# One pool of seven PSUM banks, the next batch's queries made beside attention, and its first sixteen row maxima spread over both feed-forward stretches

## The chip, the cores and the metric

The kernel runs on one core of a Trainium2 chip. The core has five engines with instruction streams of their own: TensorE (PE in the profile; its weight loads are shown as PEld), VectorE (DVE), ScalarE (ACT), GpSimd (POOL) and SyncE (SP), which here only starts DMAs. Each engine takes its instructions strictly in the order in which they were written; engines meet only through semaphores. PSUM is the memory that TensorE writes into; it has eight banks of 128 partitions x 512 float32. The metric is device time in microseconds (us) for one launch, lower is better.

## The reference, cut to what matters

Two transformer layers over 8 batches of 256 rows x 128 features. Everything is float32.

```python
# per batch b: x [256,128], ctx [1601,128], idx [256,64] in 0..255
x = x + xattn0(layernorm(x), ctx)       # 16 heads of width 8, softmax over 1601 keys
x = x + ffn0(layernorm(x))              # 9 experts of 352 hidden, sigmoid gate, top 2
x = x + xattn1(layernorm(x), ctx, idx)  # q rows attend to 64 of the first 256 latent keys each
x = x + ffn1(layernorm(x))              # 8 experts of 176 hidden, softmax gate, top 2, one shared expert
# expert: silu(x @ w1.T) * (x @ w3.T) @ w2.T, weighted per row; all experts are computed for all rows
# attn:   softmax((q * 8**-0.5) @ k.T) @ v, then an output projection
```

## The kernel before, in words

**Layer 0 attention.** Keys and queries are split into bfloat16 parts and stacked on 48 (+3) rows, so that one bfloat16 matmul gives a float32-like score. Heads are taken in pairs (p = 0 to 7), one on partitions 0 to 63 and one on 64 to 127. First the row maximum of the scores is needed. For each pair the 256 queries x 1601 keys are cut into 8 pieces, `max_part` makes the scores of a piece for both heads in two neighbouring banks (event `part`, 64 per batch, L566), and VectorE reduces both banks in one instruction (L1031). After the eighth piece of a pair VectorE takes the minimum (negated maxima), GpSimd splits it into three bfloat16 parts and writes them into the query stack `qst` (L1156 to L1159), TensorE transposes the pair's queries again (event `q0`, L535), and only then are the real scores made, keys on partitions: event `s0` (`scores`, L581, two banks, 56 per batch), exp on ScalarE (L838), weighted sum of the values in bank `ob` (event `w0`, L595), then `ev0` and `c0`.

**Layer 1 attention** does the same with 256 keys and a count mask: `pair1`, `q1`, `s1`, `mu`, `w1`, `c1` for each head pair. The counts come from `df` (GpSimd, L1197), `eq` (VectorE, L1057) and `cnt` (TensorE, L740).

**Feed-forward.** 27 chunks (layer 0) and 14 chunks (layer 1) of up to 128 hidden rows. `gu` puts the gate and up products of a chunk into the two halves of one bank (L652, L653); ScalarE makes tanh and a copy (L844, L814); VectorE makes (tanh+1)*gate and frees the bank (event `hd`, L1043); GpSimd multiplies by the up half into `hid` (L1191). `dn` (L663) multiplies an expert's hidden rows by its down weights, and VectorE adds the weighted result to x (L1049).

**What is prepared for the next batch.** `ctx`, `key`, `val`, `lat`: transposed context, keys, values. Key parts are written to DRAM and read back into the stack `kst`, two head pairs at a time (event `rel` on SyncE, L485, semaphore `kst_in0` to `kst_in3`). `n4`, `n4a`, `xT4`, `pq0`: the first layernorm, transpose and projection of the queries; VectorE makes their high parts, GpSimd the low parts (L1147 to L1150). `idx`: GpSimd turns the row indices into the form that `df` needs (L1134 to L1141). `all0` (L529): all queries transposed into `qa`, the operand of the maxima.

**What sets the order.** `order()` gives every event a time on an abstract axis and sorts; all engines walk the one sorted list and issue their share of each event. A batch takes R = 87.35 units: attention of batch b from 0 to 56 together with layer 1 attention of batch b-1; layer 1 feed-forward of b-1 from Y1 = 55; layer 0 feed-forward of b from Y0 = 65.5 to about 86. The times only set an order; they are not waits.

**Banks.** Events that ScalarE reads (`F_NEED`: `s0`, `s1`, `q0`, `q1`, `c0`, `cnt`, `ctx`, `key`, `val`, `all0`, ...) take the three banks `b0` to `b2` in strict rotation; `free_fill(e)` waits until the user three places earlier has been read. Events that VectorE reads (`M_NEED`: `part`, `pair1`, `dn`, norm transposes, ...) and `gu` take the four quarters of `um`, placed by a small planner, and `free_slot` waits for the last user. `f_read` counts ScalarE's reads, `u_read` VectorE's. In the program before, a chunk `gu` of batches 2 to 6 takes its bank a median of 2 places after the event that frees it, and a least of 1; `s0` a median of 5 and a least of 1; `part` a median of 7 and a least of 2 (places in the sorted list, all events counted).

## Time and profile before

| | us |
|---|---|
| median of 3 runs | 2027.4 (2025.6 to 2028.34) |
| profiled execution, whole | 2015.62 |
| its span | 2013.8 |
| TensorE busy | 1657.3 (82%) |
| VectorE, ScalarE, GpSimd busy | 1027.6, 985.7, 960.3 |
| mean granted TensorE clock | 0.89 of full speed |

The profile names a line of the kernel, the engine, the operation and output<-inputs with buffer numbers left out (`b` for b0 to b2; `big` is one tile that holds many small ones). "Idle before" is the time that the engine sat idle just before the instruction, and what ended it. Times inside one batch are read from the period that begins at 1126 us: layer 1 feed-forward until 1157, layer 0 feed-forward until 1218, attention until 1359; the next period begins there.

### The profile page before, as it was taken

The page shows a single profiled execution, that of the slowest core. Times are in us where ns is not written, and L with a number is a line of the kernel's source. Part 1 is how long each engine was busy: PE and PEld are TensorE (multiplying, and loading weights), DVE is VectorE, ACT ScalarE, POOL GpSimd, SP SyncE. Part 2 cuts the span into 40 slices and gives each one's busy share as a digit, 9 for nine tenths or more (in the row PEclk, how much of TensorE's full clock was granted, in tenths as well). Part 3 has the DMA queues.
Part 4 walks back from the last instruction along what each step waited for, and adds up shares of the span by engine and source line. Part 5 has one row for each costly group of instructions (what it writes and reads, how often), then busy time and mean ns, then how long its engine had stood idle before and what let it go on. Part 6 is the DMA issues. An engine that isn't in the chain of part 4 may idle for free.

```text
span 2013.8 us, 35829 instructions
## 1 busy us (share of the span) xinstructions
PE 1657.3 (82%) x13006; PEld 889.9 (44%) x13006; DVE 1027.6 (51%) x2124; ACT 985.7 (49%) x2543; POOL 960.3 (48%) x1529
## 2 busy tenths in 40 slices
PE   3488778898788988889888987889788997889667
PEld 3233543356333753347433563337533474336425
DVE  3355365545654556535665456545565446645313
ACT  2256436653467435663366445564366533663222
POOL 0345335644366345645357354654457453653342
PEclk8589888899799998889889997889988998999857
DMA  6300400021000200011000200002000200000000
GB/s 180 94 9 18 81 1 9 18 58 27 1 17 19 76 1 1 25 40 47 1 9 18 62 24 1 17 20 74 1 2 25 49 18 1 1 11 6 1 1 3
DMA packets 64863, 53.74 MB, mean 27 GB/s; under 512 B 14762, under 2 KB 57140, under 8 KB 64692
## 3 DMA queue, kind: packets, MB, share of 16 engines
q1 hardware_dynamic: 64692, 51.47, 10.2%
q8 instruction: 107, 1.75, 0.4%
q14 instruction: 64, 0.52, 0.1%
HBM read 38.98 MB, written 12.46 MB: 26 GB/s over the span
## 4 chain that ended last, share of the span: by engine, by line
PE 66%; ACT 10%; DVE 9%; POOL 8%; issue 5%; SPq 1%; DMA 1%; ACTq 0%; POOLq 0%; DVEq 0%
PE um L663 10%; PE ob L595 10%; PE um L652 7%; PE b L581 7%; PE um L566 6%; PE um L653 5%; ACT probs L838 4%; DVE mx L1031 3%; PE b L541 3%; PE b L621 2%; ACT big L814 2%; ACT big L889 2%; POOL hid L1191 2%; PE um L608 2%; PE b L637 2%
## 5 line engine op out<-in xcount | busy, mean ns | idle before, releaser
L1031 DVE TENSOR_REDUCE mx<-um 128x2 f32<-128x802 f32 (+1 forms) x512 | 502.3, 991 | 351.6 <-PE um L566 346.5
L838 ACT ACTIVATE probs<-b 128x512 f32<-128x512 f32 (+1 forms) x896 | 458.6, 564 | 185.4 <-PE b L581 176.1
L1191 POOL TENSOR_TENSOR hid<-hid,th 128x256 f32<-128x256 f32 (+3 forms) x328 | 237.5, 728 | 408.1 <-DVE th L1043 406.4
L844 ACT ACTIVATE th<-um 128x256 f32<-128x256 f32 (+3 forms) x328 | 125.6, 383 | 404.3 <-PE um L653 386.7
L595 PE MATMUL ob<-probs,vaug 128*9 128x256 f32 (+1 forms) x3328 | 305.6, 420 | 0.0
L1197 POOL TENSOR_TENSOR big<-iotab,idx_lo 128x512 bf16<-128x512 bf16 x256 | 267.6, 1058 | 23.0 <-PE b L740 16.6
L581 PE MATMUL b<-big,kst 64*128 64x256 bf16 (+1 forms) x1664 | 188.0, 299 | 83.5 <-ACT big L889 36.2
L566 PE MATMUL um<-kst,qa 64*128 64x401 bf16 (+1 forms) x1024 | 193.1, 375 | 14.6 <-DVE mx L1031 12.1
L814 ACT ACTIVATE big<-b 128x256 bf16<-128x256 bf16 (+3 forms) x280 | 104.5, 380 | 189.8 <-PE b L535 110.1
L1043 DVE SCALAR_TENSOR_TENSOR th<-th,um 128x256 f32<-128x256 f32 (+3 forms) x328 | 135.2, 414 | 102.6 <-ACT hid L814 100.4
L652 PE MATMUL um<-xnT,w1T 128*128 128x256 f32 (+1 forms) x432 | 143.1, 414 | 34.8 <-DVE th L1043 20.0
L1049 DVE SCALAR_TENSOR_TENSOR x<-um,cw,x 128x128 f32<-128x128 f32 x288 | 87.7, 346 | 164.5 <-PE um L663 164.5
L581 PEld LDWEIGHTS b<-big,kst 64*128 64x128 bf16 (+1 forms) x1664 | 64.8, 98 | 184.5 <-ACT probs L838 62.2
L663 PE MATMUL um<-w2T,hid 128*128 128x128 f32 (+1 forms) x864 | 118.2, 289 | 27.8 <-POOL hid L1191 27.8
L653 PE MATMUL um<-xnT,w3T 128*128 128x256 f32 (+1 forms) x432 | 130.5, 384 | 0.0
L663 PEld LDWEIGHTS um<-w2T,hid 128*128 128x128 f32 (+1 forms) x864 | 109.8, 201 | 39.0 <-DVE th L1043 31.5
L814 ACT ACTIVATE hid<-um 128x256 f32<-128x256 f32 (+3 forms) x328 | 123.8, 377 | 0.0
L663 PE MATMUL um<-wd_sb,hid 128*128 128x128 f32 (+1 forms) x576 | 121.3, 318 | 1.9 <-POOL hid L1191 1.9
L566 PEld LDWEIGHTS um<-kst,qa 64*128 64x128 bf16 x1024 | 52.1, 98 | 154.6 <-issue 73.0
L1221 POOL TENSOR_TENSOR big<-big 128x512 f32<-128x512 f32 (+2 forms) x40 | 35.6, 889 | 165.5 <-ACT big L814 165.5
L1119 DVE TENSOR_REDUCE mx<-um 128x4 f32<-128x1024 f32 x64 | 78.3, 1223 | 66.4 <-PE um L612 65.6
L1233 POOL TENSOR_TENSOR big<-big,sq_nat 128x512 f32<-128x512 f32 x64 | 80.2, 1274 | 57.3 <-ACT big L889 57.3
(203 smaller groups left out, 2293.1 us busy)
## 6 DMA issues: line engine op xcount, KB each, us to landing
kst<-k_parts SPq DMA_DIRECT2D x384, 50.0 KB
k_parts<-big SPq DMA_DIRECT2D x72, 128.0 KB, 1.9
ctx_sb<-in_ctx SPq DMA_DIRECT2D x8, 768.0 KB
k1st<-k_parts SPq DMA_DIRECT2D x96, 32.0 KB
k_parts<-big SPq DMA_DIRECT2D x24, 64.0 KB, 1.6
kst<-in_L_ffn_w SPq DMA_DIRECT2D x1, 1408.0 KB
x<-in_x SPq DMA_DIRECT2D x8, 128.0 KB, 2.3
out<-x SPq DMA_DIRECT2D x8, 128.0 KB, 1.8
```

Of the source, the lines that this page charges most:

```text
L566: m = pe.matmul(own[hh][:, 0:n], qa[o:o + SLOT, p, s, :], kst[o:o + SLOT, p, j * KM:j * KM + n], start=True, stop=True)
L581: m = pe.matmul(own[hh][0:kn, (c % 2) * NQ:(c % 2 + 1) * NQ], kst[o:o + SLOT, p, c * P:c * P + kn], qp[o:o + SLOT, p % 2, :], start=True, ...
L595: m = pe.matmul(ob[q:q + V1, 0:NQ], vaug[b % 2][0:kn, c, 2 * p + hh, :], probs[0:kn, (2 * (NGB * b + g) + hh) % NPS, (c % 2) * NQ:(c % 2 + ...
L652: pe.matmul(g[0:n, 0:NQ], wa, xnT[l][:, :], start=True, stop=True)
L653: pe.matmul(g[0:n, NQ:2 * NQ], wb, xnT[l][:, :], start=True, stop=True).then_inc(gu_ready, 1)
L663: m = pe.matmul(bank[:, s * P:(s + 1) * P], hid[r0:r1, (NCH * b + u) % NHID, s * P:(s + 1) * P], w[r0:r1, at, :], start=(k == 0), stop=(k ...
L814: return act.activation(o, i, ACT.Copy)
L838: act.activation(probs[0:kn, (2 * own + hh) % NPS, 0:w], bs[(e + hh) % 3][0:kn, 0:w], ACT.Exp).then_inc(f_read, 1)
L1031: dve.tensor_reduce(mx[:, p % 2, s, :, j], pair[:, :, 0:w], AX, ALU.max, negate=True).then_inc(u_read, 1)
L1043: dve.scalar_tensor_tensor(out=t, in0=t, scalar=1.0, in1=g[0:nr, 0:NQ], op0=ALU.add, op1=ALU.mult).then_inc(u_read, 1)
L1191: pool.tensor_tensor(hid[0:nr, own % NHID, :], hid[0:nr, own % NHID, :], th[0:nr, own % NTH, :], ALU.mult).then_inc(hid_ready, 1)
L1197: m = pool.tensor_tensor(onehot[:, own % 2, q:q + QG, :], iotab[:, :].unsqueeze(1).to_broadcast([P, QG, P]), idx_lo[:, QG * n:QG * (n + 1) ...
```

## The change

Four edits go together.

1. `um` has 3584 columns, seven banks, and `b0` to `b2` are gone. One planner walks the sorted list and gives every event the bank or banks whose last user was released longest ago; an event that needs two banks for one VectorE instruction (`part`, `pair1`) must get neighbours. A bank counts as ready when its last user's event (for `gu`: its `hd`) lies earlier in the list. `free_bank` then waits on `f_read`, on `u_read`, or on both, for the last users of just these banks.
2. `n4`, `n4a`, `xT4`, `pq0`, `all0` and `idx` of the next batch move from the layer 0 feed-forward (Y0+1.0 to Y0+9.7) into attention (36.2 to 51.5).
3. The first 16 maxima of the next batch (12 before) are spread evenly from Y1+1.4 = 56.4 to 84.9, one per 1.90 units; before, the 12 came one per 0.82 units from 77.4 on. The other 48 come one per 0.896 units from 0.1 on (52, one per 0.82, before).
4. ScalarE's reads take the bank from the plan.

By the new plan `gu` takes its bank a median of 7 places after the event that frees it (least 6), `s0` 6 (least 4), `part` 6 (least 3), `s1` 6 (least 5; before 3, least 2). Of the 56 `s0` of batch 4, 26 now wait for a VectorE read too, and of all events that waited only for ScalarE's reads 51 do; of its 64 `part` 29 now wait for a ScalarE read.

```diff
-        um = psum("um", 2048)
-        bs = [psum(f"b{k}", 512) for k in range(3)]
+        um = psum("um", 512 * NBANK)
...
+        EARLY = 16
+        EARLY_STEP = (R - 2.4 - Y1 - 1.4) / (EARLY - 1)
...
-                for d, kind in ((1.0, "n4"), (2.5, "n4a"), (3.3, "xT4"), (4.6, "idx"), (4.8, "pq0"), (12.1, "lat")):
-                    put(prep + Y0 + d, kind, b)
+                for d, kind in ((36.2, "n4"), (37.8, "n4a"), (38.6, "xT4"), (45.6, "pq0"), (51.5, "idx"), (Y0 + 12.1, "lat")):
+                    put(prep + d, kind, b)
-                    put(prep + Y0 + 9.1 + 0.6 * n, "all0", b, n)
+                    put(prep + 50.2 + 0.7 * n, "all0", b, n)
-                    put(own - 9.9 + 0.82 * k if k < 12 else own + 0.82 * (k - 12) + 0.1, "part", b, k)
+                    put(prep + Y1 + 1.4 + EARLY_STEP * k if k < EARLY else own + (43.0 / (NH0 - EARLY)) * (k - EARLY) + 0.1, "part", b, k)
...
+            need = F_NEED.get(kind, 0) or M_NEED.get(kind, 0) or int(kind == "gu")
...
+            ready = [k for k in range(NBANK) if since(k) < at[ev]]
+            if kind in M_NEED and need == 2:
+                own = min(([k, k + 1] for k in ready if k + 1 in ready), key=lambda r: max(since(k) for k in r))
+            else:
+                own = sorted(ready, key=since)[:need]
+            place[ev] = own
+            before = [last[k] for k in own if last[k] is not None]
+            f_free[ev] = max([fill[v] + F_NEED[v[0]] for v in before if v in fill], default=0)
+            u_free[ev] = max([rel[v] + 1 for v in before if v not in fill], default=0)
...
-            def free_fill(e):
-                if e >= 3:
-                    pe.wait_ge(f_read, e - 2)
-                return bs[e % 3][:, :]
-
-            def free_slot(ev):
+            def free_bank(ev):
+                if f_free[ev] > 0:
+                    pe.wait_ge(f_read, f_free[ev])
                 if u_free[ev] > 0:
                     pe.wait_ge(u_read, u_free[ev])
                 return quarter[place[ev][0]]
```

Three places of the order. TensorE, in the second half of the layer 0 feed-forward of batch 4, before; one expert is three chunks `gu` (w1T, w3T) and one `dn` (w2T), and `um<-kst,qa` is a maximum of the next batch:

```order
1933 L652 MATMUL um<-xnT,w1T 96x256
1934 L653 MATMUL um<-xnT,w3T 96x256
1935 L566 MATMUL um<-kst,qa 128x401 x2
1936 L652 MATMUL um<-xnT,w1T 128x256
1937 L653 MATMUL um<-xnT,w3T 128x256
1938 L566 MATMUL um<-kst,qa 128x401 x2
1939 L652 MATMUL um<-xnT,w1T 128x256
1940 L653 MATMUL um<-xnT,w3T 128x256
1941 L566 MATMUL um<-kst,qa 128x401 x2
1942 L663 MATMUL um<-w2T,hid 128x128 x6
```

The same engine and stretch now:

```order
1948 L662 MATMUL um<-xnT,w1T 96x256
1949 L663 MATMUL um<-xnT,w3T 96x256
1950 L576 MATMUL um<-kst,qa 128x401 x2
1951 L662 MATMUL um<-xnT,w1T 128x256
1952 L663 MATMUL um<-xnT,w3T 128x256
1953 L662 MATMUL um<-xnT,w1T 128x256
1954 L663 MATMUL um<-xnT,w3T 128x256
1955 L673 MATMUL um<-w2T,hid 128x128 x6
```

One maximum stands in each expert instead of three in the last four experts. GpSimd in the layer 0 feed-forward of batch 4, before, with `idx` and the low parts of the next queries between two chunks' products:

```order
748 L1191 TENSOR_TENSOR hid<-hid,th 96x256
749 L1134 TENSOR_SCALAR idx_f<-idx_t 128x128
750 L1137 CAST idx_c<-idx_f 64x128
751 L1138 TENSOR_SCALAR idx_c<-idx_t 64x128
752 L1137 CAST idx_c<-idx_f 64x128
753 L1138 TENSOR_SCALAR idx_c<-idx_t 64x128
754 L1140 TENSOR_SCALAR idx_f<-idx_f 128x128
755 L1141 TENSOR_TENSOR idx_lo<-idx_t,idx_f 128x128
756 L1147 CAST qst<-qres 128x32x8
757 L1148 TENSOR_TENSOR qst<-qres,qst 128x32x8
758 L1149 COPY qst<-qst 128x32x16
759 L1150 COPY qst<-qst 128x32x8
```

GpSimd now, at the end of attention of batch 4; the last rows of `key` (L1231 to L1235) and `df` (L1207) stand between them:

```order
726 L1207 TENSOR_TENSOR big<-iotab,idx_lo 128x512 x2
727 L1157 CAST qst<-qres 128x32x8
728 L1158 TENSOR_TENSOR qst<-qres,qst 128x32x8
729 L1159 COPY qst<-qst 128x32x16
730 L1160 COPY qst<-qst 128x32x8
731 L1231 TENSOR_TENSOR big<-big 128x256
732 L1233 CAST big<-big 128x256
733 L1235 TENSOR_TENSOR big<-big 128x256
734 L1207 TENSOR_TENSOR big<-iotab,idx_lo 128x512
```

The low parts now stand ahead of the last key of the batch, whose parts go to DRAM. TensorE at the start of the layer 1 feed-forward (wg_sb, wu_sb), beside the last sums of attention, before:

```order
3881 L652 MATMUL um<-xnT,wg_sb 128x256 [waits u_read]
3882 L653 MATMUL um<-xnT,wu_sb 128x256
3883 L595 MATMUL ob<-probs,vaug 9x256 [waits f_read]
3884 L595 MATMUL ob<-probs,vaug 9x256 x3
3885 L652 MATMUL um<-xnT,wg_sb 128x256 [waits u_read]
3886 L653 MATMUL um<-xnT,wu_sb 128x256
```

And now:

```order
3203 L662 MATMUL um<-xnT,wg_sb 128x256 [waits f_read]
3204 L663 MATMUL um<-xnT,wu_sb 128x256
3205 L605 MATMUL ob<-probs,vaug 9x256 [waits f_read]
3206 L605 MATMUL ob<-probs,vaug 9x256 x3
3207 L576 MATMUL um<-kst,qa 128x401 [waits f_read,kst_in0]
3208 L576 MATMUL um<-kst,qa 128x401
3209 L662 MATMUL um<-xnT,wg_sb 128x256 [waits f_read]
```

The first maximum of the next batch, with its wait for the first key stack, stands here now; before it stood about 21 units later. (The two excerpts are of different batches; the pattern is the same in each.)

## Rows read from the trace of the kernel before

**Rows 1.** The page, parts 1 and 4: busy time, and the last chain by engine.
```profile
PE 1657.3 (82%) x13006; PEld 889.9 (44%) x13006; DVE 1027.6 (51%) x2124; ACT 985.7 (49%) x2543; POOL 960.3 (48%) x1529
...
PE 66%; ACT 10%; DVE 9%; POOL 8%; issue 5%; SPq 1%; DMA 1%; ACTq 0%; POOLq 0%; DVEq 0%
```
**Rows 2.** Windows: length, busy of PE, PEld, DVE, ACT, POOL, clock, DMA share, GB/s.
```profile
1126.00:1157.00 31.00, 30.64 (x166) 21.16 (x158) 16.81 (x74) 11.15 (x35) 9.39 (x13) 1.00 0.35 75
1157.00:1218.00 61.00, 51.90 (x305) 39.55 (x306) 32.73 (x77) 22.16 (x62) 30.28 (x48) 0.97 0.07 20
1218.00:1359.00 141.00, 118.38 (x1108) 46.31 (x1109) 76.06 (x108) 86.07 (x214) 80.18 (x128) 0.83 0.04 13
```
**Rows 3.** Waits of PE, whole run: waiting <- releaser: us, times, longest.
```profile
PE b L535 <- POOL qst L1159: 43.4, 24, 2.5
PE b L581 <- ACT big L889: 36.2, 43, 1.0
...
PE um L663 <- POOL hid L1191: 29.8, 23, 2.8
...
PE um L652 <- DVE th L1043: 20.4, 37, 1.4
...
PE b L581 <- ACT probs L838: 16.9, 46, 0.5
PE b L581 <- ACTq L866: 15.4, 19, 1.4
PE b L621 <- ACT probs L838: 15.0, 26, 0.8
PE um L652 <- DVE x L1049: 14.8, 21, 0.7
PE um L566 <- DVE mx L1031: 12.1, 18, 1.1
```
**Rows 4.** Waits of PE's weight loads, whole run.
```profile
PEld b L581 <- ACT probs L838: 62.2, 119, 0.9
...
PEld b L581 <- ACT big L889: 46.3, 43, 1.3
```
**Rows 5.** Timeline, layer 0 feed-forward: start, us, engine, line, operation.
```profile
1169.35 0.54 POOL L1134 TENSOR_SCALAR idx_f<-idx_t 128x128 f32<-128x128 f32 x1
...
1175.91 2.77 POOL L1191 TENSOR_TENSOR hid<-hid,th 128x256 f32<-128x256 f32 x4
...
1178.14 1.58 PE L663 MATMUL um<-w2T,hid 128*128 128x128 f32 x12 [2.81 <-POOL hid L1191]
```
**Rows 6.** Timeline, attention: a pair's maximum ready, its transpose.
```profile
1053.68 0.22 POOL L1159 TENSOR_TENSOR qst<-nmr,qst 128x4 bf16<-128x4 f32 x1
...
1054.04 0.27 PE L535 MATMUL b<-identb,qst 128*128 128x128 bf16 x2 [0.91 <-POOL qst L1159]
```
**Rows 7.** The page, part 5: a maximum on VectorE.
```profile
L1031 DVE TENSOR_REDUCE mx<-um 128x2 f32<-128x802 f32 (+1 forms) x512 | 502.3, 991 | 351.6 <-PE um L566 346.5
```
**Rows 8.** Tile kst from 1110 to 1200 us: issues, ns min/median/max, first and last start.
```profile
L485 SPq DMA_DIRECT2D kst<-k_parts x48: 265/298/593, 1123.8 to 1140.1; - x48
```
**Rows 9.** The page, part 6: DMA issues and KB each.
```profile
kst<-k_parts SPq DMA_DIRECT2D x384, 50.0 KB
...
k1st<-k_parts SPq DMA_DIRECT2D x96, 32.0 KB
```
**Rows 10.** Windows of that stretch, columns as in Rows 2.
```profile
1119.00:1124.00 5.00, 4.19 (x50) 2.11 (x46) 2.06 (x10) 3.79 (x10) 0.70 (x1) 1.00 0.25 71
1124.00:1130.00 6.00, 5.69 (x56) 2.45 (x53) 2.91 (x22) 4.12 (x11) 0.73 (x1) 1.00 0.51 104
```
**Rows 11.** Timeline of PE and PEld in the layer 1 feed-forward.
```profile
1129.12 0.62 PE L595 MATMUL ob<-probs,vaug 128*9 128x256 f32 x8
...
1154.36 0.41 PEld L653 LDWEIGHTS um<-xnT,wu_sb 128*128 128x128 f32 x2
...
1154.79 1.65 PEld L663 LDWEIGHTS um<-wd_sb,hid 128*128 128x128 f32 x8
```

More of the change, by code:

```diff
@@ L156, in build @@
         cw = [sb("cw0", [P, NS, NE]), sb("cw1", [P, NS, NE])]
-        um = psum("um", 2048)
-        bs = [psum(f"b{k}", 512) for k in range(3)]
+        um = psum("um", 512 * NBANK)
         ob = psum("ob", 512)
-        quarter = [um[:, 512 * k:512 * (k + 1)] for k in range(4)]
+        quarter = [um[:, 512 * k:512 * (k + 1)] for k in range(NBANK)]
         def sem(name):
@@ L367, in build, with since @@
                 serial[ev] = (group, 1 + sum(1 for g in serial.values() if g[0] == group))
-        seen, last = 0, [-1] * 4
+        at = {ev: k for k, ev in enumerate(EV)}
+        given = {ev: at["hd", ev[1], ev[2]] if ev[0] == "gu" else at[ev] for ev in EV}
+        last = [None] * NBANK
+        f_free, u_free = {}, {}
         for ev in EV:
             kind = ev[0]
-            if kind in M_NEED or kind == "gu":
-                need = M_NEED.get(kind, 1)
-                at = [range(k, k + need) for k in range(5 - need) if max(last[k:k + need]) < seen]
-                own = min(at, key=lambda r: (kind == "gu" and last[r[0] ^ 1] < seen, max(last[k] for k in r)))
-                u_free[ev] = max(last[k] for k in own) + 1
-                place[ev] = list(own)
-                for k in own:
-                    last[k] = rel[ev]
-            if kind in M_NEED or kind == "hd":
-                seen += 1
+            need = F_NEED.get(kind, 0) or M_NEED.get(kind, 0) or int(kind == "gu")
+            if not need:
+                continue
+            def since(k):
+                return -1 if last[k] is None else given[last[k]]
+            ready = [k for k in range(NBANK) if since(k) < at[ev]]
[3 more added lines that the diff above has]
+                own = sorted(ready, key=since)[:need]
+            assert len(own) == need, ev
+            place[ev] = own
+            before = [last[k] for k in own if last[k] is not None]
+            f_free[ev] = max([fill[v] + F_NEED[v[0]] for v in before if v in fill], default=0)
+            u_free[ev] = max([rel[v] + 1 for v in before if v not in fill], default=0)
+            for k in own:
+                last[k] = ev
         count = {ev: n for ev, (group, n) in serial.items()}
@@ L570, in scores @@
                 p, j = divmod(g, NG)
-                e = fill["s0", b, g]
                 if j == 0:
                     pe.wait_ge(f_read, fill["q0", b, p] + 1)
-                own = [free_fill(e), free_fill(e + 1)]
+                free_bank(("s0", b, g))
+                own = [quarter[k] for k in place["s0", b, g]]
                 if b == 0:
@@ L616, in scores1 @@
             def scores1(b, p):
-                e = fill["s1", b, p]
                 pe.wait_ge(f_read, fill["q1", b, p] + 1)
-                own = [free_fill(e), free_fill(e + 1)]
+                free_bank(("s1", b, p))
+                own = [quarter[k] for k in place["s1", b, p]]
                 for hh in range(2):
@@ L724, in _ @@
                 elif kind == "all0":
-                    bank = free_fill(fill[ev])
+                    bank = free_bank(ev)
                     pe.wait_ge(qst_ready, b + 1)
@@ L728, in _ @@
                 elif kind == "q0":
-                    bank = free_fill(fill[ev])
+                    bank = free_bank(ev)
                     pe.wait_ge(m_ready, NP * b + n + 1)
@@ L742, in _ @@
                 elif kind == "xT4":
-                    bank = free_slot(ev)
+                    bank = free_bank(ev)
                     pe.wait_ge(ln_ready, norm_no("n4", b))
@@ L759, in _ @@
                 elif kind == "aT0":
-                    bank = free_slot(ev)
+                    bank = free_bank(ev)
                     pe.wait_ge(at_ready, b + 1)
@@ L763, in _ @@
                 elif kind == "o0":
-                    bank = free_slot(ev)
+                    bank = free_bank(ev)
                     pe.wait_ge(u_read, rel["aT0", b, 0] + 1)
@@ L779, in _ @@
                 elif kind == "all1":
-                    bank = free_fill(fill[ev])
+                    bank = free_bank(ev)
                     pe.wait_ge(qst1_ready, b + 1)
@@ L797, in _ @@
                 elif kind == "aT1":
-                    bank = free_slot(ev)
+                    bank = free_bank(ev)
                     pe.wait_ge(at1_ready, b + 1)
@@ L801, in _ @@
                 elif kind == "o1":
-                    bank = free_slot(ev)
+                    bank = free_bank(ev)
                     pe.wait_ge(u_read, rel["aT1", b, 0] + 1)
@@ L827, in _ @@
                     e = fill[ev]
-                    bank = bs[e % 3][:, :]
+                    bank = quarter[place[ev][0]]
                     act.wait_ge(f_psum, e + 1)
@@ L837, in _ @@
                         act.wait_ge(f_psum, e + hh + 1)
-                        act.activation(probs[0:kn, (2 * own + hh) % NPS, 0:w], bs[(e + hh) % 3][0:kn, 0:w], ACT.Exp).then_inc(f_read, 1)
+                        act.activation(probs[0:kn, (2 * own + hh) % NPS, 0:w], quarter[place[ev][hh]][0:kn, 0:w], ACT.Exp).then_inc(f_read, 1)
                 elif kind == "gu":
```

45 lines of the change are left out of this document (23 added, 22 removed).

## The prediction

> **What bounds the kernel now.** I read the page first, then the windows of one batch, then who waited for whom on TensorE.
>
> The page shows no engine near its limit but TensorE: busy 82% of the span, the other three 48 to 51%, and the chain that ended last runs through TensorE for 66% of the span [rows 1]. So the question is what makes TensorE stand idle. The three windows of one batch (233 us) answer where: layer 1 feed-forward is dense (30.6 of 31 us busy), layer 0 feed-forward is idle for 61 - 51.9 = 9.1 us, attention for 141 - 118.4 = 22.6 us [rows 2]. The batch has 200.9 us of busy TensorE and 32.1 us of idle. The granted clock is 1.00 and 0.97 in the feed-forward windows and 0.83 in attention.
>
> The waits say why. Seven rows are waits for a bank: scores for ScalarE's exp and copies (36.2, 16.9, 15.4 us), layer 1 scores (15.0), feed-forward chunks for VectorE (20.4, 14.8), maxima for VectorE (12.1); together 130.8 us [rows 3]. They go with places in the order: a chunk's bank is freed one or two events before it is taken, a score's sometimes one. Two rows are waits for data: a pair's queries for GpSimd's maximum parts (43.4) and the down product for GpSimd's hidden rows (29.8) [rows 3].
>
> **The change part by part.** The sum is over the whole run and against the profiled execution's own 2015.6 us; the median of the runs is 2027.4, 11.8 higher, and I carry the difference over to it.
>
> *Seven banks in one pool.* At most the 130.8 us of idle go, if nothing else is late. The weight loads show that each such wait also lays bare the tail of the matmul before it: for the scores they waited 62.2 + 46.3 = 108.5 us where the matmuls' rows of the same two releasers show 16.9 + 36.2 = 53.1 [rows 3, 4]. With the whole of the scores' three wait rows (68.5) set against 108.5, the factor is 1.58, and the upper end is 130.8 x 1.58 = 207 us. The lower end is below nothing, since scores now also wait for VectorE (the rival below). After the change every kind has 6 to 7 events between free and take, at 2.5 us per score group in attention (141 us for 56) the six events are more than one group, about 3 us, against 1 us for a maximum on VectorE [rows 7] and twice 0.6 for the exps. That holds most of the time, not always, because ScalarE and VectorE also run in order and some waits will come back as waits for data a little later. I take 0.7 of the idle: -92 us.
>
> *Maxima spread.* Before, the last maximum of pair 1 (k = 15) stood at 0.82 x 3 + 0.1 = 2.6 units and the pair's queries at 2.8; pair 2's at 9.1 against 9.8. VectorE, four GpSimd steps and a semaphore had to fit between them, and TensorE waited: in the row at 1054 us it starts 0.14 us after GpSimd's last step ended [rows 6]. Now pair 1 is done before attention starts, pair 2 at 6.4 against 9.8, pair 7 at 42.2 against 44.8: always 2.6 units or more, 6 us. The 43.4 us [rows 3] go except for a rest; I take -40 (ends -20 and -43). The four maxima that leave attention are the same work elsewhere: no change in the sum of TensorE.
>
> *Next queries beside attention.* In the feed-forward GpSimd spends 1169.35 to 1175.91, 6.6 us, on `idx` and the low parts while four chunk products pile up behind it; the down product waits 2.81 us for them [rows 5]. Eight times 2.8 is 22 us of the 29.8; I take -20 (ends 0 and -22). In attention the same 6.6 us lie beside other work: GpSimd is busy 80 of 141 us there [rows 2], and all queries are needed 4.6 units after the projection. TensorE's transposes and projection only change place. If that cover were gone, the next `all0` would wait, at most 6.6 us a batch.
>
> *The first maximum waits for the stack.* `kst` of the first two pairs is read back by 12 DMAs that start at 1123.8, behind 12 of `k1st` [rows 8]. Together these are 12 x 32 + 12 x 50 = 984 KB [rows 9]; the traffic from 1119 to 1130 is 71 x 5 + 104 x 6 = 979 KB [rows 10]. So the stack is there at about 1130.0 or a little later. The new first maximum stands behind the sum at 1129.12 [rows 11], so about 1129.7: 0.3 us early. Moreover the low parts now stand ahead of the last key on GpSimd, and the reload hangs on that key. If none of it shifts, the wait is 0.3; if the whole 6.6 us block came before the key it would be 6.9. Both engines meet work there that partly overlaps, so I take 1.5 us a batch, +12 us (ends 0 and +55). Behind the waiting matmul stand all chunks of the dense layer 1 feed-forward, and VectorE's `hd` behind the missing maximum.
>
> *Five maxima inside the layer 1 feed-forward.* TensorE has no idle there [rows 2]; VectorE has 14 us. A 0.99 us maximum [rows 7] that stands in front of an `hd` can make a down product late. One of five does, I assume: 1.0 x 8 = +8 us (ends 0 and 5 x 0.99 x 8 = +40).
>
> *A second semaphore.* Some 50 scores and other fills a batch now wait for two. A down product has always waited for two: at 1154.79 its weights load 0.02 us after the load before it ended (1154.36 + 0.41) [rows 11]. I take 0; a tenth of a us each would be +40.
>
> Sum: -92 - 40 - 20 + 12 + 8 = -132 us: 1883.6 for the profiled execution, 1895 for the median. Per batch it is 16.5 us of the 32.1 idle. The layer 0 feed-forward window should go from 61 to about 52 us: up to 9.1 of idle there, less what returns, and the queries' projection and transposes moved out.
>
> **The rivals.**
>
> *The waits only change their names.* Every score still needs its exp before the sum, and ScalarE, VectorE and GpSimd take 86, 76 and 80 of attention's 141 us in order [rows 2]. If that chain sets the pace, a score that starts earlier only waits in front of the sum. Then only the feed-forward's bank waits go (20.4 + 14.8 = 35), half of the 43.4 and the 20, against +20: -57, 1970. For it: layer 1's chain of eight steps per pair is fixed latency. Against it: no engine there is over 61% busy, and the scores' waits name the bank's reader, not the data.
>
> *The clock comes back.* Attention has 0.83, so about 34% of its time at 1.2 GHz and the rest at 2.4 (0.66 + 0.34/2), and the feed-forward windows, where TensorE hardly pauses, have 0.97 to 1.00 [rows 2]. The clock fell where pauses are many. If the pool closes most of them, up to 48 us a batch run at full clock; with TensorE busy for 84% of it, half of 40 us is saved at most, and other engines take half of that again: 10 us a batch, -80 on top, 1815. Against it: sums that are short for the array remain, so pauses remain. The Trainium skill, "TensorE: Matmul & The Clock Gate", section on psum-queue depth-cycling, tells of a kernel that cycles through PSUM banks with small idles between matmul groups, whose clock swings between the two levels and whose throughput falls; by it fewer waits for banks would give this result. The trace agrees in that clock and idle go together by window.
>
> *Slower: scores held by maxima.* One pool ties ScalarE's banks to VectorE's. In a batch 51 events that waited for ScalarE alone now wait for a VectorE read as well. If VectorE lags more than a score group behind (a norm, a routing block, `eq` in a row), each holds TensorE for up to one maximum, 0.99 us [rows 7]: 50 us a batch at most. Set against it, what the change takes away is (130.8 + 43.4 + 22) / 8 = 24.5 us a batch, so it decides from 25 of the 51 on. At 31 it costs 6 us a batch more than is gained: 2075. Against it: VectorE is busy for 54% of attention and waited 346.5 us for maxima itself [rows 2, 7], so it is usually ahead.
>
> **How the numbers follow.** My forecast has 0.62, from its terms between 1840 and 1950. The renamed waits have 0.17 (1970, 1950 to 2015), the returning clock 0.10 (1815), the slower case 0.11 (2075). The range 1825 to 1990 leaves out the slower case, a piece of the renamed waits and a piece of the clock's, together 2 in 10. A difference under 0.2% (4 us) is about what a measurement of this kernel can't tell from none. Faster by more: 0.62 + 0.10 + 0.14 of the 0.17 = 0.86; within: 0.03; slower: 0.11.
>
> **What would show it.** In the profile after: the waits of scores (now L591) for ScalarE and VectorE together under 40 us, of pair queries (L548) for GpSimd under 5, of chunks (L662) for VectorE under 10; the layer 0 feed-forward window at 50 to 54 us; the first maximum waiting for a DMA of `kst` for 0 to 3 us in each batch; TensorE's busy sum per batch near 200 us, unless the clock changes. The prediction is wrong if waits of the sums (L605) for exps grow by as much as the scores' fall, if scores wait for `mx` for tens of us, or if attention stays at 140 us.

## The result, and the profile after

The changed kernel takes 1903.66 us (median of 3 runs, 1889.44 to 1908.15) against 2027.4: a ratio of 0.9375, 95% interval 0.9297 to 0.9453. The forecast was 1895. Times further down are medians that leave out an execution over 1.5% above the fastest of its kernel. The profiled execution spans 1901.8 us. The page after, answering to [rows 1]:

```profile
PE 1616.2 (85%) x13006; PEld 884.1 (46%) x13006; DVE 1023.9 (54%) x2124; ACT 971.0 (51%) x2543; POOL 957.6 (50%) x1529
...
PE 60%; POOL 10%; DVE 9%; ACT 8%; issue 5%; SPq 4%; DMA 3%; POOLq 0%; ACTq 0%; DVEq 0%
```

The span fell by 112 us, in two parts: TensorE's idle from 2013.8 - 1657.3 = 356.5 to 1901.8 - 1616.2 = 285.6 (-71), and its busy time by 41, though it does the same 13006 matmuls. A DMA has come onto the chain (3%, with SyncE's queue 4%). The windows of one batch, answering to [rows 2]; lengths differ since the stages were cut at their first chunks:

```profile
1061.00:1100.00 39.00, 34.22 (x176) 22.84 (x169) 21.11 (x77) 11.40 (x37) 9.46 (x13) 0.91 0.24 66
1100.00:1148.00 48.00, 45.68 (x268) 35.16 (x268) 27.41 (x63) 19.40 (x57) 20.34 (x31) 1.00 0.09 25
1148.00:1285.00 137.00, 120.03 (x1175) 49.60 (x1173) 76.87 (x124) 89.39 (x224) 89.64 (x145) 0.86 0.05 15
```

One batch is a sample; for comparisons I cut every profile at the first and last layer 0 chunk and the first layer 1 chunk and took the mean over six batches. "Slow" is the time at 1.2 GHz that the mean granted clock c stands for, length x 2(1 - c); c is read to two digits, so it is good to about half a us.

| kernel | layer 1 feed-forward | layer 0 feed-forward | attention | of it idle | of it slow | batch |
|---|---|---|---|---|---|---|
| before | 31.3 | 55.4 | 144.4 | 24.8 | 36.4 | 231.1 |
| after | 39.2 | 47.6 | 130.8 | 16.8 | 23.5 | 217.6 |

So the two feed-forward stages nearly cancel (+7.9 and -7.8), and what is left is attention (-13.6), of whose gain 8.0 us are idle and up to half of 12.9 the clock. TensorE's waits after, answering to [rows 3]:

```profile
PE um L576 <- DMA kst<-k_parts: 38.2, 8, 6.9
PE um L673 <- POOL hid L1201: 32.7, 18, 3.1
...
PE um L647 <- POOL big L1243: 23.8, 18, 3.5
...
PE um L554 <- ACT oT L824: 20.9, 27, 1.5
PE um L548 <- POOL big L1169: 16.0, 16, 2.5
PE um L591 <- DVE mx L1041: 15.2, 18, 1.2
PE um L618 <- ACT probs L848: 9.9, 18, 0.8
...
PE um L591 <- ACT big L899: 4.4, 15, 0.5
PE um L591 <- ACT probs L848: 4.1, 12, 0.6
...
PE um L576 <- DVE mx L1041: 4.0, 11, 0.6
```

The scores (L581, now L591) waited for ScalarE for 36.2 + 16.9 + 15.4 us; now it is 8.5, and 15.2 for a maximum on VectorE. Chunks (L652, now L662) have no wait row left, and the wait of layer 0's pair queries for `qst` (43.4) is gone; the 16.0 at L548 are layer 1's (`big`), which were 2.9. New at the top is the key stack's DMA, once in each batch. This is the place, TensorE at the start of the layer 1 feed-forward (start, us, engine, line, operation):

```profile
1064.05 0.62 PE L605 MATMUL ob<-probs,vaug 128*9 128x256 f32 x8
1069.33 0.52 PE L576 MATMUL um<-kst,qa 64*128 64x401 bf16 x2 [4.66 <-DMA kst<-k_parts]
1069.77 1.22 PE L662 MATMUL um<-xnT,wg_sb 128*128 128x256 f32 x2
1070.78 1.06 PE L663 MATMUL um<-xnT,wu_sb 128*128 128x256 f32 x2
1071.64 1.06 PE L662 MATMUL um<-xnT,wg_sb 128*112 128x256 f32 x2
```

The first maximum waits for 4.66 us, and behind it the same product takes 1.06 instead of 0.59 us. The granted clock was 1.00 from 1060.6 to 1064.7, fell during the pause, and was 0.50, the lower level, for 4.2 us behind it:

```profile
1069.30:1073.50 4.20, 4.17 (x12) 2.54 (x14) 1.74 (x3) 0.66 (x2) 1.15 (x2) 0.50 0.52 182
```

From 1075 to 1080 it was 1.00 again. The reload before the pause, GpSimd and SyncE in the same stretch:

```profile
1050.53 0.48 POOL L1160 COPY qst<-qst 128x256 bf16<-128x256 bf16 x1
1050.98 0.67 POOL L1231 TENSOR_TENSOR big<-big 128x256 f32<-128x256 f32 x1
...
1056.39 4.11 SPq L486 DMA_DIRECT2D k1st<-k_parts  x12
1060.61 3.68 SPq L498 DMA_DIRECT2D kst<-k_parts  x11
```

GpSimd's work on the last key (L1231) starts only when the low parts of the next queries are done (L1160), then comes the `k1st` reload, then the one that the maximum needs.

### The profile page after: what moved, and what is told of

Its sections match the earlier page's. It is cut to its first block, busy times and chain, and to the rows that moved or that the text cites. A ratio compares the mean times of both kernels' runs of the same rounds, so it can differ in the third digit from the quotient of the medians.

```text
span 1901.8 us, 35726 instructions
## 1 busy us (share of the span) xinstructions
PE 1616.2 (85%) x13006; PEld 884.1 (46%) x13006; DVE 1023.9 (54%) x2124; ACT 971.0 (51%) x2543; POOL 957.6 (50%) x1529
## 4 chain that ended last, share of the span: by engine, by line
PE 60%; POOL 10%; DVE 9%; ACT 8%; issue 5%; SPq 4%; DMA 3%; POOLq 0%; ACTq 0%; DVEq 0%
PE um L673 11%; PE ob L605 8%; PE um L662 7%; PE um L663 6%; PE um L576 5%; PE um L591 4%; DVE mx L1041 3%; PE um L554 3%; ACT probs L848 3%; POOL big L1243 3%; DMA kst<-k_parts 2%; PE um L631 2%; PE um L647 2%; SPq L498 2%; ACT big L824 1%
## 5 line engine op out<-in xcount | busy, mean ns | idle before, releaser
L848 ACT ACTIVATE probs<-um 128x512 f32<-128x512 f32 (+1 forms) x896 | 459.1, 571 | 141.4 <-PE um L591 134.7
L605 PE MATMUL ob<-probs,vaug 128*9 128x256 f32 (+1 forms) x3328 | 297.8, 408 | 0.0
L1207 POOL TENSOR_TENSOR big<-iotab,idx_lo 128x512 bf16<-128x512 bf16 x256 | 266.0, 1053 | 10.6 <-PE um L750 4.4
L576 PE MATMUL um<-kst,qa 64*128 64x401 bf16 (+1 forms) x1024 | 187.1, 362 | 57.3 <-DMA kst<-k_parts 38.2
L591 PE MATMUL um<-big,kst 64*128 64x256 bf16 (+1 forms) x1664 | 180.0, 291 | 26.7 <-DVE mx L1041 15.2
L824 ACT ACTIVATE big<-um 128x256 bf16<-128x256 bf16 (+3 forms) x280 | 105.3, 383 | 135.0 <-PE um L647 51.1
L673 PE MATMUL um<-w2T,hid 128*128 128x128 f32 (+1 forms) x864 | 114.3, 282 | 37.5 <-POOL hid L1201 29.8
L662 PE MATMUL um<-xnT,w1T 128*128 128x256 f32 (+1 forms) x432 | 136.5, 398 | 0.0
L673 PEld LDWEIGHTS um<-w2T,hid 128*128 128x128 f32 (+1 forms) x864 | 104.4, 193 | 54.6 <-issue 30.3
L663 PE MATMUL um<-xnT,w3T 128*128 128x256 f32 (+1 forms) x432 | 129.3, 381 | 0.0
L673 PE MATMUL um<-wd_sb,hid 128*128 128x128 f32 (+1 forms) x576 | 125.6, 326 | 3.5 <-POOL hid L1201 2.9
L1129 DVE TENSOR_REDUCE mx<-um 128x4 f32<-128x1024 f32 x64 | 78.2, 1221 | 78.6 <-PE um L622 78.6
L591 PEld LDWEIGHTS um<-big,kst 64*128 64x128 bf16 (+1 forms) x1664 | 61.2, 98 | 115.2 <-ACT probs L848 48.4
L673 PEld LDWEIGHTS um<-wd_sb,hid 128*128 128x128 f32 (+1 forms) x576 | 89.4, 192 | 43.9 <-issue 12.0
```

Source lines behind the costliest of these rows:

```text
L576: m = pe.matmul(own[hh][:, 0:n], qa[o:o + SLOT, p, s, :], kst[o:o + SLOT, p, j * KM:j * KM + n], start=True, stop=True)
L591: m = pe.matmul(own[hh][0:kn, (c % 2) * NQ:(c % 2 + 1) * NQ], kst[o:o + SLOT, p, c * P:c * P + kn], qp[o:o + SLOT, p % 2, :], start=True, ...
L605: m = pe.matmul(ob[q:q + V1, 0:NQ], vaug[b % 2][0:kn, c, 2 * p + hh, :], probs[0:kn, (2 * (NGB * b + g) + hh) % NPS, (c % 2) * NQ:(c % 2 + ...
L662: pe.matmul(g[0:n, 0:NQ], wa, xnT[l][:, :], start=True, stop=True)
L663: pe.matmul(g[0:n, NQ:2 * NQ], wb, xnT[l][:, :], start=True, stop=True).then_inc(gu_ready, 1)
L673: m = pe.matmul(bank[:, s * P:(s + 1) * P], hid[r0:r1, (NCH * b + u) % NHID, s * P:(s + 1) * P], w[r0:r1, at, :], start=(k == 0), stop=(k ...
```

## The experiments

All are timed against the kernel before; the ratios are to it, with 95% intervals. "Pool" is the seven-bank planner, "queries" the next queries beside attention, "spread" the early maxima spread. One thing in their profiles has to be allowed for: each shows 67 fewer of these matmuls than the profiles before and after (12939 of 13006), mostly the first of the two mask products ahead of layer 1's scores. Taking the like records out of the profiles before and after moves 13.1 and 12.4 us there from busy to idle (before: 1644.2 busy and 369.6 idle; after: 1603.8 and 298.0). Idle and busy sums of the whole run are compared with these below.

| kernel | us | ratio |
|---|---|---|
| pool only | 1917.33 | 0.9465 (0.9424 to 0.9506) |
| queries + spread, old banks | 2087.68 | 1.0292 (1.0232 to 1.0352) |
| queries, old banks | 2006.37 | 0.9894 (0.9845 to 0.9943) |
| pool + queries | 1873.94 | 0.9252 (0.9205 to 0.9299) |
| pool + queries + spread (the change) | 1903.66 | 0.9375 (0.9297 to 0.9453) |
| the change with six banks | 1928.57 | 0.9542 (0.948 to 0.9605) |
| the change, stack reload first | 1851.22 | 0.915 (0.9112 to 0.9187) |
| the change, maxima from 61.4 | 1838.48 | 0.9086 (0.9049 to 0.9123) |
| both of these, halfway | 1871.05 | 0.9242 (0.9198 to 0.9285) |
| maxima from 61.4, last down later | 1829.09 | 0.903 (0.8985 to 0.9075) |
| the same, queries behind the last key | 1829.43 | 0.9017 (0.8982 to 0.9052) |
| the same as last down later, fillers in all batches | 1852.68 | 0.9136 (0.9096 to 0.9175) |
| the same, fillers in every fourth group | 1835.05 | 0.9046 (0.8988 to 0.9105) |

**Pool only.** The planner of the changed kernel with the old order:

```diff
-                for d, kind in ((36.2, "n4"), (37.8, "n4a"), (38.6, "xT4"), (45.6, "pq0"), (51.5, "idx"), (Y0 + 12.1, "lat")):
-                    put(prep + d, kind, b)
+                for d, kind in ((1.0, "n4"), (2.5, "n4a"), (3.3, "xT4"), (4.6, "idx"), (4.8, "pq0"), (12.1, "lat")):
+                    put(prep + Y0 + d, kind, b)
-                    put(prep + 50.2 + 0.7 * n, "all0", b, n)
+                    put(prep + Y0 + 9.1 + 0.6 * n, "all0", b, n)
-                    put(prep + Y1 + 1.4 + EARLY_STEP * k if k < EARLY else own + (43.0 / (NH0 - EARLY)) * (k - EARLY) + 0.1, "part", b, k)
+                    put(own - 9.9 + 0.82 * k if k < 12 else own + 0.82 * (k - 12) + 0.1, "part", b, k)
```

> The seven-bank pool alone: the order of events is that of the kernel before (12 early maxima 0.82 units apart, next queries in the layer 0 feed-forward), the planner and waits are those of the changed kernel. My theory (bank waits were 92 of the 132 us forecast, and of the 124 measured): scores, layer 1 scores and chunks stop waiting for banks, the 43 us of pair queries waiting for GpSimd and the 2.8 us per batch behind the GpSimd block stay, no wait for the key stack: 1930 to 1945. Rival (waits only change their names; the order edits carried the gain): 1980 to 2000, with the waits of the sums for exps, or of combines, grown by what the scores lost.

1917, below the expected range: 109 us under the before of its own job (2025.9) with no other edit. Its waits:

```profile
PE um L548 <- POOL qst L1169: 51.5, 29, 2.5
PE um L673 <- POOL hid L1201: 33.2, 24, 2.8
...
PE um L554 <- ACT oT L824: 18.7, 25, 1.5
PE um L576 <- DVE mx L1041: 15.7, 23, 1.5
PE um L673 <- DVE mx L1041: 13.4, 7, 1.9
PE um L591 <- DVE mx L1041: 8.8, 8, 1.3
PE um L591 <- ACT probs L848: 8.5, 24, 0.6
```

As the theory had it, the chunks' waits are gone, the scores' are a third of what they were (78.6 to 26.0 in all their rows), and the pair queries' wait stays. Combines (L554) did take some over: 18.7 where before they waited 3.6 for `oT`. In the profile idle fell by 70 us (369.6 to 1925.2 - 1626.1 = 299.1) and busy time by 18 (1644.2 to 1626.1), at a mean granted clock of 0.88 where it was 0.89. These 88 us are less than 109 because the profiled execution here took longer than the median (1927.0 against 1917.3) and the one before took less (2015.6 against 2027.4).

**Queries and spread on the old banks.** The same order edits, all four pairs of lines above taken the other way, in the kernel before.

> The order edits alone: banks and waits of the kernel before, order of the changed kernel. My theory: pair queries no longer wait for GpSimd (-43), the GpSimd block leaves the feed-forward (-20), the first maximum waits for the key stack as it did in the changed kernel (38 us of TensorE idle and some slow clock behind it), bank waits stay near 130 us: 1995 to 2025, nearly nothing. Rival (order carries the gain): 1900 to 1940. If both e1 and e2 gain more than half, the two parts overlap; if their sum is less than the whole, the pool needs the new order.

2088, slower by 62 us: both expectations were wrong. The layer 1 feed-forward is 47.7 us instead of 31.3 (its mean over six batches); the window of one and a row in it:

```profile
1163.00:1213.00 50.00, 44.33 (x169) 29.17 (x169) 20.90 (x72) 10.44 (x34) 10.20 (x14) 0.70 0.17 40
```

```profile
1182.57 0.70 PE L654 MATMUL um<-xnT,wg_sb 128*128 128x256 f32 x2 [2.30 <-DVE mx L1033]
```

A maximum takes two of the four quarters that chunks and down products share, and the next chunk stands for VectorE's reduction of it; the clock there is 0.70. The wait for the DMA was only 9.3 us, which fits a TensorE that comes late itself.

**Queries alone on the old banks.** The first three of these pairs of lines in the kernel before.

> The kernel before (banks three and four) with only the next queries moved beside attention; the maxima stay where they were. Order-only, which also spreads the maxima, was slower than before by 69 us. Theory: that loss is the spread maxima, which take two of the four quarters among the chunks of the dense layer 1 feed-forward (chunks there waited up to 2.3 us for VectorE's maximum; the stage took 47.7 us instead of 31.3); moving the queries alone gains 20 to 45: 1983 to 2007. Rival (the moved queries themselves crowd the three banks of attention): 2030 to 2080.

2006, within the expected 1983 to 2007. Layer 1 feed-forward is back at 31.6 us. So on the old banks the queries gain some 20 us and the spread loses some 80. The down products' wait for GpSimd (L663 for `hid`) is 10.2 us, where it was 29.8; idle is 16 us less (353.4), and the time at the slow clock in attention is as before (36.4 us a batch).

**Pool and queries, old maxima.** Only the last of these pairs of lines, in the changed kernel.

> The seven-bank pool and the next queries beside attention, but the maxima as in the kernel before (12 early ones, 0.82 units apart, from 77.4). Against the pool alone (1917) this tells what moving the queries is worth. Theory: the 2.8 us behind the GpSimd block and about 2 us of moved work leave the layer 0 feed-forward, attention grows by the moved work, the pair queries' 50 us wait for GpSimd stays: 1895 to 1905. Rival (moving them puts GpSimd's low parts in front of keys and count masks and costs as much): 1912 to 1925.

1874, better than I had expected: 43 us under pool only and 30 under the full change. Its layer 0 feed-forward is 46.4 us (52.8 with the pool alone) and attention did not grow (135.8 against 137.3). It keeps its wait of pair queries for GpSimd, and its down products' wait for `hid` is 12.3 us where the pool alone had 33.2:

```profile
PE um L548 <- POOL qst L1169: 51.5, 29, 2.5
...
PE um L673 <- POOL hid L1201: 12.3, 17, 2.1
```

Attention's idle is the same in both (21.0 and 20.8 us a batch), but it has 27.8 us at the slow clock against 35.9, and the layer 0 feed-forward none against 4.6. Over the whole run idle is 16 us less (283.2), and busy time 38 less (1588.0).

**Six banks**, in the changed kernel:

```diff
-NBANK = 7
+NBANK = 6
```

> The changed kernel with NBANK = 6, one bank left unused. It tells the sharing from the number: before there were seven banks too, but split three and four. Theory (a bank taken by age out of one pool is what counts, distances go from 6 or 7 events to 5): 1915 to 1950, still far under 2027. Rival (seven is just enough; with six the neighbours that a maximum needs are often not free): 1960 to 2030.

1929, within the expected range: with the same order edits six banks in one pool beat seven in two by 159 us (2087.7) and lose 25 to seven in one. So the pool matters more than the number of banks. What in it does, the sharing itself, the choice by age or the waits for just the bank's last user, isn't told apart: no run gives a split set of banks the new planner. The mechanism isn't only the one of the theory either: much of the waiting came back (334.5 us of idle, where the change has 298.0), but attention has only 14.2 us a batch at the slow clock, against 23.5, and over the whole run its busy time is lower (1592.1 against 1603.8). Why it has the better clock with more idle, these runs don't tell.

**The stack reload first.**

```diff
-                    put(prep + (48 if c < 3 else XL + 1.5), "rel", b, c)
+                    put(prep + (46.4 if c == 0 else 48 if c < 3 else XL + 1.5), "rel", b, c)
```

> The changed kernel with one event moved: the reload of the first two head pairs' key stack is issued at 46.4 units, ahead of the batch's last (layer 1) key and its reload, not at 48 behind them. Theory: the wait of the first maximum for this DMA (38 us in all, up to 6.9 each) goes, and with it the half-speed clock of about 4 us that follows each (1.06 against 0.59 us for a product): 1850 to 1865. Rival (slack elsewhere: the chain nm0 to rt0 or VectorE sets when the layer 0 feed-forward starts, so TensorE only waits later): 1890 to 1905.

1851. The DMA holds TensorE once, for 4.9 us in the first batch, where it was 6.2; the seven waits of the later batches are gone, 33.3 us in all. The layer 1 feed-forward is dense at full clock, 31.9 us instead of 39.2, and the other two stages are as long as in the change (47.6 and 130.6 us), so the whole gain lies at the pause: over the run 33 us of idle (264.8 against 298.0) and 21 of busy time (1582.6 against 1603.8). The window of one batch:

```profile
1024.00:1056.00 32.00, 31.88 (x172) 21.86 (x170) 21.11 (x78) 11.07 (x35) 9.47 (x13) 1.00 0.22 59
```

**Maxima later.**

```diff
-        EARLY_STEP = (R - 2.4 - Y1 - 1.4) / (EARLY - 1)
+        EARLY_STEP = (R - 2.4 - Y1 - 6.4) / (EARLY - 1)
-                    put(prep + Y1 + 1.4 + EARLY_STEP * k if k < EARLY else own + (43.0 / (NH0 - EARLY)) * (k - EARLY) + 0.1, "part", b, k)
+                    put(prep + Y1 + 6.4 + EARLY_STEP * k if k < EARLY else own + (43.0 / (NH0 - EARLY)) * (k - EARLY) + 0.1, "part", b, k)
```

> The changed kernel with the first early maximum at 61.4 units, not 56.4; the sixteenth stays at 84.9, so they are 1.57 units apart. Theory: as for the stack-first kernel the DMA wait goes: 1855 to 1875, a little worse than it since there are more maxima per expert in the layer 0 feed-forward (VectorE 0.99 us each in front of the chunks' step). Rival (the even spread from the start is what made the feed-forward fast): 1900 or more.

1838, below the expected range: 65 us less than the change by moving 16 of its 64 maxima. Here the DMA holds TensorE only in the first two batches (3.9 and 1.8 us). Two quite different edits that end its regular wait gain 52 and 65 us, which is the test of that cause. The first gives its price cleanly; in the second attention is shorter too (20.9 us at the slow clock a batch against 23.5), so not all of the 65 is the wait's.

**Both, halfway.** The stack reload first, and the maxima from 58.9:

```diff
-                    put(prep + (48 if c < 3 else XL + 1.5), "rel", b, c)
+                    put(prep + (46.4 if c == 0 else 48 if c < 3 else XL + 1.5), "rel", b, c)
-        EARLY_STEP = (R - 2.4 - Y1 - 1.4) / (EARLY - 1)
+        EARLY_STEP = (R - 2.4 - Y1 - 3.9) / (EARLY - 1)
```

> The changed kernel with the first stack reload at 46.4 as in stack-first (1851) and the first maximum at 58.9 (halfway). In stack-first the DMA still held the first maximum once for 4.9 us, in later-maxima twice for 5.7 in all. Theory: neither waits now: 1832 to 1842, like later-maxima. Rival (later-maxima is faster than stack-first because maxima near the start disturb the dense layer 1 feed-forward by themselves, not through the DMA): 1842 to 1852.

1871, outside both expectations, and 33 us slower than maxima later. The regular DMA wait is gone here too (5.9 us, in the first batch only), so the third edit that ends it gains just 33. Attention is 4.5 us a batch longer than in maxima later. It is not idle: TensorE's idle in attention is 18.1 us a batch here and 18.3 there, but 34.5 us are at the slow clock against 20.9. Attention of one batch in both, this kernel first:

```profile
1121.00:1260.00 139.00, 120.36 (x1169) 51.17 (x1177) 77.54 (x125) 89.84 (x225) 89.60 (x145) 0.85 0.07 20
```

```profile
1309.00:1440.00 131.00, 113.98 (x1168) 48.87 (x1175) 76.82 (x124) 89.35 (x225) 88.92 (x143) 0.91 0.05 16
```

The same number of matmuls is busy for 6.4 us longer at 0.85 than at 0.91. Why the granted clock differs between two orders with the same idle, these runs don't tell.

**The last down product later.** In the changed kernel and in maxima later TensorE waits at the end of layer 0 for GpSimd's last hidden rows, and then works at half speed (2.90 us instead of 1.57 for a down product), here in maxima later:

```profile
1105.01 2.90 PE L673 MATMUL um<-w2T,hid 128*128 128x128 f32 x12 [3.05 <-POOL hid L1201]
```

The edit is made in maxima later:

```diff
-                    put(own + Y0 + CL * (J0 * e + 2) + 2.2, "dn", b, e)
+                    put(own + Y0 + CL * (J0 * e + 2) + (2.2 if e < NE - 1 else 2.8), "dn", b, e)
```

> The later-maxima kernel (1838) with one event moved: the ninth down product of layer 0 stands at Y0 + 22.3 units instead of 21.7, so that the first score group of the next attention comes ahead of it on TensorE. In the changed kernel TensorE waits there for GpSimd's last hidden rows, 3.05 us, and runs at half speed behind it. Theory: 1.5 to 3 us a batch and some clock: 1815 to 1828. Rival (layer 1 attention's start hangs on that down product, so the time comes back behind it): 1836 to 1845.

1829, just above the expected range. The first scores fill part of the wait:

```profile
1097.40 0.39 PE L591 MATMUL um<-big,kst 64*128 64x256 bf16 x4 [0.91 <-ACT big L824]
1099.55 1.57 PE L673 MATMUL um<-w2T,hid 128*128 128x128 f32 x12 [1.59 <-POOL hid L1201]
1101.24 0.38 PE L591 MATMUL um<-big,kst 64*128 64x256 bf16 x4
1103.73 0.39 PE L591 MATMUL um<-big,kst 64*128 64x256 bf16 x4 [1.94 <-DVE mx L1041]
```

The down product is at full speed now, but 1.94 us come back two groups later.

**Queries behind the last key**, in the kernel above:

```diff
-                for d, kind in ((36.2, "n4"), (37.8, "n4a"), (38.6, "xT4"), (45.6, "pq0"), (51.5, "idx"), (Y0 + 12.1, "lat")):
+                for d, kind in ((36.2, "n4"), (37.8, "n4a"), (38.6, "xT4"), (46.7, "pq0"), (51.5, "idx"), (Y0 + 12.1, "lat")):
```

> The last-down kernel (1829) with the projection pq0 at 46.7 instead of 45.6 units, behind the last key, so that GpSimd's low parts no longer stand ahead of that key's parts (1.4 us in the changed kernel). The first maximum's wait for the DMA there was 7.0 in two pieces. Theory: this wait goes to 0 to 3, little else: 1820 to 1829. Rival (all0 then waits for the low parts, or the clock in attention falls differently): 1832 to 1850.

1829.4, between the two expectations and within a us of the kernel above. The wait for the DMA did not go to 0 to 3 us as expected but only from 7.0 to 6.3: 5.9 of it is in the first batch (5.3 before), and that of the second fell from 1.6 to 0.5. The later batches had no such wait left to lose, so the 1.4 us that the low parts held up the key no longer matter once the first maximum stands later.

**Fillers.** Ahead of each score group of the first batch the kernel puts one filler matmul, a 128 x 512 bfloat16 product into the scores' own bank, which the scores then overwrite. Here the last-down kernel has it in all batches:

```diff
-                if b == 0:
-                    keep_clock(1, own[0])
+                keep_clock(1, own[0])
```

> The last-down kernel (1829) with the filler matmul that batch 0 has (one 128 x 512 bfloat16 product into the score's own bank ahead of each score group) in all batches, 448 instead of 56. It writes what the scores then overwrite, so nothing computed changes. It asks whether attention's slow clock (20 us of it per batch at half speed in the last-down kernel, 35 in the one with both shifts, which has the same idle but is 33 us slower than later-maxima) is a cost that can be bought back. Theory: each filler takes 0.2 us of TensorE, 12 us a batch at most, part of it in idle time; the clock goes to 0.97 or more in attention and gives back 20 x 0.85 / 2 = 8.5 us: 1815 to 1870, about even. Rival (clock is only a symptom of idle, fillers are pure load): 1900 or more.

And in every fourth score group:

```diff
-                if b == 0:
+                if b == 0 or g % 4 == 0:
```

> The last-down kernel (1829) with a filler in every fourth score group of batches 1 to 7 instead of all (which raised attention's clock from 0.923 to 0.988 and took 6 of 17 us idle, but added 10 us of busy TensorE a batch, 1853). Theory: about 14 fillers a batch, 3 us of load at most, and if they fall into idle they buy back part of the 20 us of slow clock: 1815 to 1832. Rival (too few to hold the clock up, only load): 1833 to 1850.

1853, inside the expected range but a loss of 24 us, and 1835. With all fillers attention's slow time falls from 20.1 to 3.1 us a batch and its idle from 17.4 to 9.9, and it is still 131.1 us long against 128.9, in the profile of an execution of 1843.6 us: TensorE is busy for 121.2 us instead of 111.5. The window of one batch:

```profile
1103.00:1236.00 133.00, 122.65 (x1224) 50.93 (x1231) 77.20 (x127) 89.49 (x225) 89.43 (x145) 0.99 0.06 17
```

The second lies in the rival's range, but its interval overlaps that of 1829, so between these two nothing is shown. So the clock can be held up, but neither number of fillers gains here.

## Why the prediction was right

The size came out (-124 against -132), and so did the main step, that most of what bank waits cost goes with one pool. That the total came so close is partly luck. Pool and queries were forecast at -112 and gave -153 (2027 to 1874); spread, stack wait and the five maxima were forecast at -20 together and gave +30 (1874 to 1904). Errors of 41 and 50 us cancel. The sum has no term for the clock, and both errors lie there in good part. Term by term:

*Seven banks in one pool*, forecast -92 of idle: right, and a little small; the pool alone gave -109. The waits of scores, layer 1 scores, chunks and maxima together were 144.8 us in all their rows, of which [rows 3] shows the 130.8, and are 56.3 with the pool alone, a fall of 88. Idle as a whole fell by 70, as some of it came back under other names. Busy time fell by 18 at no better clock, which is what the weight loads' rows had hinted at [rows 4]: with a wait gone the next matmul starts inside the tail of the last. It is a quarter of the idle, not the 0.58 that the upper end had.

*Maxima spread*, forecast -40 (ends -20 and -43): right in that the 51.5 us wait of the pair queries goes, but the time is less sure. Against pool + queries, three kernels have the spread without the regular DMA wait: maxima later is 36 us faster, stack first 23, and both, halfway only 3. Their idle is less by 31, 18 and 22 us, and what the clock does in attention adds to it or takes it away (20.9, 22.8 and 34.5 us slow a batch against 27.8).

*Next queries beside attention*, forecast -20: right for the wait that it named, and short by the clock. The down products' wait for `hid` fell by 20 on the old banks (29.8 to 10.2) and by 21 on the pool (33.2 to 12.3), and idle as a whole by 16 in both. On the old banks the time fell by some 20. On the pool it fell by 43, since busy time fell by 38 as well, with about 100 us less at the slow clock in the profiles (454 to 352, the span times 2(1 - c) with c of 0.882 and 0.906). The fall on the pool is clear of the noise; why the clock improved with the queries there and not on the old banks is open. In the full change GpSimd's wait came back elsewhere: the row of 29.8 is now 32.7, 1.4 us a batch near the start of the stage and 2.0 to 3.1 at its end, where two maxima and a pair's queries used to stand between the last chunk and the last down product, and one pair's queries stand alone now.

*The first maximum waits for the stack*, forecast +12 with ends 0 and +55: the term that was mis-sized. It measured 38.2 us of idle, and without the seven regular waits (33.3 us less of this row) the time is 52 us less. From the last key's matmul to the landing the estimate of [rows 10] makes 17.8 us (1112.2 to 1130.0), and it took about 21.3 (1048.0 to 1069.3): 1.4 for the low parts ahead of the key, and 2.5 between the first `kst` DMA's issue and the landing (8.7 us where I had 6.2), with 0.3 won between. I had taken the stack to be there when the traffic added up to its 984 KB. But from 1056.4 to the landing at 1069.3 the DMA engines moved 94 x 12.9 = 1213 KB, so other traffic, by its place most likely the reloads issued behind, went through ahead of the stack's end. TensorE also reached the maximum 0.8 us sooner after that key's matmul (16.7 us against 17.5). And I had left out what a pause of 4.7 us does to the clock: 21 of the 52 us or so are busy time.

*Five maxima in the layer 1 feed-forward*, forecast +8 for products that come late: not seen. With the stack first TensorE is idle there for 0.1 us a batch, as with the pool alone. The stage is 31.9 us against 30.3, but these 1.6 us are the maxima's own work, which has left the other stages.

*A second semaphore*, forecast 0: not measured apart; the dense stage shows nothing of it (31.88 of 32 us busy).

The rivals. *The waits only change their names* holds in part: combines for `oT` 20.9 (3.6 before), layer 1 queries 16.0 (2.9), layer 1 sums 23.8 (17.3), together 37 us, where the bank waits fell from 144.8 to 45.0 and the pair queries' lost 43.4: a quarter. *The clock comes back*: attention's slow time fell by 13 us a batch, 36.4 to 23.5; half of it is the worth at most, 6 us a batch. So this rival holds in part as well, and the layer 1 feed-forward gives back about half of it with the 7 us a batch that it now has at the slow clock. With fillers, buying the rest cost more than it brought. The Trainium skill, "TensorE: Matmul & The Clock Gate", section on psum-queue depth-cycling, tells of a clock that swings where TensorE is often briefly idle while it goes through its banks. By that fewer bank waits should mean a better clock. The pool + queries kernel agrees (27.8 us slow against 36.4 in attention); the pool alone does not (35.9), though it has most of the gain, and six banks does not, with more idle than the change and 14.2 us slow. *Scores held by maxima*: 15.2 us in 18 waits in the whole run, where it needed 25 waits a batch; it did not happen. A slower case did exist, and I had not seen it: the spread without the pool.

Of the signs that I had named, the scores' waits (25.9 us in all rows) and the chunks' (none) came as said. Three did not: the layer 0 feed-forward is shorter than 50 to 54 us (47.6), the first maximum waits for longer than 3 us (3.3 to 6.9), and the pair queries wait 16.0 us for GpSimd, not under 5, all of it layer 1's.

## What to carry to other kernels

Before adding buffers, look whether the ones there are split by reader: one pool taken by age, each bank with its own wait, gave 109 us here, and with the order of the change six banks in one pool kept 159 of the 184 us that seven have over the split. Work that holds up a dense stage on another engine is worth moving out of it: the wait that it caused lost 20 us on either bank scheme. When work is moved earlier, every DMA it needs must be followed from its trigger to its landing, with the queue in front of it and what is issued behind it. The order edits were worth -14 us on one buffer scheme (1917 to 1904, with intervals that overlap) and +62 on the other, so parts have to be tested alone and together.

## What the runs showed that I had not expected

A single pause of 4.66 us in a dense stretch halved TensorE's clock behind it, 1.06 against 0.59 us a product for some 4 us. So an idle row understates such a pause: with 33.3 us of them gone the kernel was 52 us faster, 1.6 times as much.

Two orders with the same idle in attention (18.1 and 18.3 us a batch) had 34.5 and 20.9 us of slow clock, and 33 us of total time between them, with runs that agree to 3 us; six banks had more idle (23.2) and only 14.2. The granted clock is a result of its own in such comparisons, and an edit can lose or win by it alone.
